# Weighted values of two heads as two 64-column tiles of TensorE, softmax sums from probability tiles that GpSimd adds in pairs

## The reference, cut to what matters

```python
def xattn(q, k, v):                 # q = layernorm(x); k = v = ctx; split in 8 heads of 64
    qn, kn = l2norm(q), l2norm(k)
    sm = softmax(5.0 * einsum('bhdq,bhdk->bhqk', qn, kn), axis=-1)
    return einsum('bhqk,bhdk->bhdq', sm, v)

x = x + xattn(layernorm(x), ctx, ctx)
x = x + experts(layernorm(x))       # top 2 of 4, capacity 512, gelu, two matmuls each
```

## Time and profile before

| | |
|---|---|
| median of 3 runs | 658.95 us (657.25 to 659.49) |
| the profiled execution, its time | 659.4 us |
| its span, first to last instruction | 657.6 us |
| busy: PE, DVE, ACT, POOL | 589.5, 373.2, 300.5, 173.9 us |
| attention | about 6 to 234 us of the span |
| routing, then experts | about 234 to 285 us, then to the end |

### The profile page before, as it was taken

One profiled execution on the slowest core, in us unless ns is written; L12 is line 12 of the kernel. 1 busy time (PEld: TensorE's weight loads), 2 busy tenths in 40 slices (PEclk: granted clock), 3 DMA queues, 4 the chain that ended last, 5 costly groups with the idle time before them and its releaser, 6 DMA issues.

```text
span 657.6 us, 8090 instructions
## 1 busy us (share of the span) xinstructions
PE 589.5 (90%) x2714; PEld 429.0 (65%) x2714; DVE 373.2 (57%) x631; ACT 300.5 (46%) x454; POOL 173.9 (26%) x139
## 2 busy tenths in 40 slices
PE   1999999999999830189999999999999999999994
PEld 1555555565556430168888888888888888888883
DVE  4678888888888798843434443254524344433312
ACT  2687767776777443033434343432424243434310
POOL 4534554355434052261000053000270000320002
PEclk9999999999999965569999999999999999999998
DMA  3512122211210122045131355213272313351001
GB/s 122 175 52 95 64 80 84 92 64 65 91 69 34 64 73 87 17 118 187 64 129 65 115 185 192 84 64 124 99 270 80 128 64 127 130 184 72 1 0 64
DMA packets 39636, 63.62 MB, mean 97 GB/s; under 512 B 3520, under 2 KB 20032, under 8 KB 39616
## 3 DMA queue, kind: packets, MB, share of 16 engines
q1 hardware_dynamic: 35776, 50.78, 22.5%
q0 software_dynamic: 3840, 12.59, 5.5%
HBM read 50.77 MB, written 12.58 MB: 96 GB/s over the span
## 4 chain that ended last, share of the span: by engine, by line
PE 73%; DVE 13%; issue 4%; ACT 2%; POOL 1%; DMA 1%; DVEq 0%; POOLq 0%
PE two L1278 27%; PE two L1144 10%; PE four L1305 9%; PE four L1307 9%; PE four L1308 9%; PE four L1134 4%; DVE p_inv L759 3%; PE bank_t L1161 1%; PE bank_t L1113 1%; DVE junk L923 1%; PE bank_m L1121 1%; DVE o_norm L767 1%; DVE x_all L769 1%; PE bank_t L1153 1%; DVE ss L720 1%
## 5 line engine op out<-in xcount | busy, mean ns | idle before, releaser
L674 ACT ACTIVATE h_f<-two 128x512 f32<-128x512 f32 x64 | 38.3, 599 | 230.1 <-PE two L1278 230.1
L1081 DVE TENSOR_TENSOR h_lo<-h_f,h_hi 128x512 fp32r<-128x512 f32 x64 | 44.1, 690 | 138.7 <-ACT h_hi L675 138.6
L1144 PE MATMUL two<-prob,v_t 128*128 128x512 f32 x256 | 116.7, 598 | 0.0
L1278 PE MATMUL two<-xt_hi,w_hi 128*128 (+1 forms) x256 | 102.7, 401 | 0.3 <-ACT xt_hi L663 0.3
L1278 PE MATMUL two<-xt_hi,w_lo 128*128 (+1 forms) x256 | 101.2, 395 | 0.0
L1278 PE MATMUL two<-xt_lo,w_hi 128*128 (+1 forms) x256 | 100.7, 395 | 0.0
L1305 PE MATMUL four<-w_hi,h_hi 128*128 128x512 f32 x256 | 100.6, 393 | 0.0
L1308 PE MATMUL four<-w_hi,h_lo 128*128 128x512 f32 x256 | 100.5, 393 | 0.0
L1307 PE MATMUL four<-w_lo,h_hi 128*128 128x512 f32 x256 | 100.4, 392 | 0.0
L538 POOL DMA_INDIRECT out<-o_got,idx_all x16 | 19.7, 1232 | 297.6 <-DVE o_got L1095 295.1
L1049 DVE TENSOR_TENSOR w_lo<-raw,w_hi 128x2048 fp32r<-128x2048 f32 x30 | 68.7, 2291 | 22.2 <-ACT w_hi L637 20.0
(11 more groups left out here) (163 smaller groups left out, 727.4 us busy)
## 6 DMA issues: line engine op xcount, KB each, us to landing
raw<-in_L_ffn_W SPq DMA_DIRECT2D x64, 512.0 KB
x_all<-in_x SPq DMA_DIRECT2D x16, 256.0 KB, 2.8
c_sb<-in_ctx SPq DMA_DIRECT2D x16, 256.0 KB, 2.8
out<-x_all SPq DMA_DIRECT2D x16, 256.0 KB, 2.0
x2n_dram<-x2n SPq DMA_DIRECT2D x16, 256.0 KB, 2.1
cst<-in_consts SPq DMA_DIRECT2D x1, 354.5 KB, 4.6
x_got<-x2n_dram,idx_all POOLq DMA_INDIRECT x16
o_got<-out,idx_all POOLq DMA_INDIRECT x16
```

Source lines behind the costliest of these rows:

```text
L674: nc.scalar.activation(h_f[m % 2][:, :], z_ps[m % 2][:, :], ACT.Gelu)
L1081: nc.vector.tensor_tensor(h_lo[m % 2][:, :], h_f[m % 2][:, :], h_hi[m % 2][:, :].bitcast(F32), ALU.subtract).then_inc(h_split, 1)
L1144: last = nc.tensor.matmul(o_ps[h][:, :], v_t[u[1]][:, t, 2 * h:2 * h + 2, :] .rearrange("p a d -> p (a d)"), prob[h][t][:, :], start=(t == ...
L1278: return nc.tensor.matmul(z[:, :], w_part[c][:, w], x_k, start=start, stop=stop)
```

## The change

- The stationary operand of a head is now its 64 columns of values alone. The two heads are two column tiles of TensorE: head 0 writes partitions 0 to 63 and head 1 partitions 64 to 127 of one PSUM bank, `o_ps[0]`. The columns of ones and the memsets that set them are gone.
- GpSimd adds, for each head, probability tiles 0 and 1, then 2 and 3 (`half_sums`, four additions of 128x512 a unit). TensorE multiplies a tile of ones of 64 columns with these (`sums`, four fp32 matmuls a unit) into `o_ps[1]`, at the end of its unit.
- `take_o` is one copy in place of four; `invert_sums` reads PSUM.
- New waits: GpSimd's additions wait for `exp_done` and, into a used buffer, for the last `sums`; `sums` waits for the additions and for the last inversion; ScalarE's exponentials wait for the additions that read the buffer they overwrite. TensorE waits for all constants at its start.
- On GpSimd the additions stand ahead of `key_norms` and behind it, and `query_norms` moves ahead of `key_remainders`.
- Six `tensor_scalar` of VectorE become `scalar_tensor_tensor` with a second tensor operand: both normalisations (a broadcast `rstd`), both `var_e`, both floors.

```diff
+            def half_sums(u, n, reused):
+                pool.wait_ge(exp_done, TT * number(u) + 2 * n + 2)
+                if reused:
+                    pool.wait_ge(sums_ready, number(u))
+                for h in range(2):
+                    last = nc.gpsimd.tensor_tensor(half_sum[h][n][:, :], prob[h][2 * n][:, :],
+                                                   prob[h][2 * n + 1][:, :], ALU.add)
+                last.then_inc(halves_done, 1)
...
             def unit(u, behind, ahead):
+                half_sums(u, 0, behind > 0)
                 if ahead:
...
                     key_norms(after(u))
+                half_sums(u, 1, behind > 0)
                 if ahead > 1:
+                    query_norms(after(after(u)))
                     key_remainders(after(after(u)))
-                    query_norms(after(after(u)))
...
                 if reused:
                     act.wait_ge(pv_done, g - TT + 1)
+                    act.wait_ge(halves_done, 2 * (number(u) - 1) + t // 2 + 1)
...
-                nc.scalar.activation(p_sum[0:DH, :], o_ps[0][DH:P, :], ACT.Copy)
-                nc.scalar.activation(o_sb[0:DH, :], o_ps[0][0:DH, :], ACT.Copy).then_inc(o_taken[0], 1)
-                nc.scalar.activation(p_sum[DH:P, :], o_ps[1][0:DH, :], ACT.Copy).then_inc(sum_taken, 1)
-                nc.scalar.activation(o_sb[DH:P, :], o_ps[1][DH:P, :], ACT.Copy).then_inc(o_taken[1], 1)
+                nc.scalar.activation(o_sb[:, :], o_ps[0][:, :], ACT.Copy).then_inc(o_taken, 1)
...
-                nc.vector.tensor_scalar(var_e[:, :], mv[:, 1:2], LN_EPS, None, ALU.add).then_inc(var_done, 1)
+                nc.vector.scalar_tensor_tensor(var_e[:, :], mv[:, 1:2], LN_EPS, mv[:, 1:2], ALU.add, ALU.max
+                                               ).then_inc(var_done, 1)
...
-                nc.vector.tensor_scalar(x_norm[:, :], x_all[:, bass.ds(n, 1), :].rearrange("p a d -> p (a d)"),
-                                        mv[:, 0:1], rstd[:, 0:1], ALU.subtract, ALU.mult).then_inc(xn_done, 1)
+                nc.vector.scalar_tensor_tensor(x_norm[:, :], x_all[:, bass.ds(n, 1), :].rearrange("p a d -> p (a d)"),
+                                               mv[:, 0:1], rstd[:, 0:1].broadcast_to([P, D]), ALU.subtract, ALU.mult
+                                               ).then_inc(xn_done, 1)
...
-                dve.wait_ge(sum_taken, n + 1)
-                nc.vector.reciprocal(p_inv[:, :], p_sum[:, :]).then_inc(inv_done, 1)
+                dve.wait_ge(sums_ready, n + 1)
+                nc.vector.reciprocal(p_inv[:, :], o_ps[1][:, :]).then_inc(inv_done, 1)
...
                 for h in range(2):
-                    if reused:
-                        pe.wait_ge(o_taken[h], number(u))
-                    last = nc.tensor.matmul(o_ps[h][:, :], v_t[u[1]][:, t, 2 * h:2 * h + 2, :]
-                                            .rearrange("p a d -> p (a d)"), prob[h][t][:, :],
+                    last = nc.tensor.matmul(o_ps[0][DH * h:DH * (h + 1), :], v_t[u[1]][:, t, h, :], prob[h][t][:, :],
                                             start=(t == 0), stop=(t == TT - 1))
                 last.then_inc(pv_done, 1)
+
+            def sums(u, reused):
+                pe.wait_ge(halves_done, 2 * (number(u) + 1))
+                if reused:
+                    pe.wait_ge(inv_done, number(u))
+                for n in range(2):
+                    for h in range(2):
+                        last = nc.tensor.matmul(o_ps[1][DH * h:DH * (h + 1), :], cst[:, C_ONES:C_ONES + DH],
+                                                half_sum[h][n][:, :], start=(n == 0), stop=(n == 1))
+                last.then_inc(sums_ready, 1)
...
             pe.wait_ge(ident_in, 16)
+            pe.wait_ge(cst_in, 16)
...
                 weighted_values(u, 2)
                 weighted_values(u, 3)
+                sums(u, behind > 0)
```

More of the change, by code:

```diff
@@ L178, in xattn_moe_kernel @@
             q_lo = [att(f"q_lo{n}", [P, D], F32R) for n in range(2)]
-            v_t = [att(f"v_t{n}", [P, TT, 4, DH]) for n in range(2)]
+            v_t = [att(f"v_t{n}", [P, TT, 2, DH]) for n in range(2)]
             prob = [[att(f"prob{h}{n}", [P, D]) for n in range(TT)] for h in range(2)]
             o_sb = att("o_sb", [P, D])
-            p_sum = att("p_sum", [P, D])
+            half_sum = [[att(f"half_sum{h}{n}", [P, D]) for n in range(2)] for h in range(2)]
             p_inv = att("p_inv", [P, D])
@@ L262, in xattn_moe_kernel @@
         pv_done = sem("pv_done")
-        sum_taken = sem("sum_taken")
-        o_taken = [sem(f"o_taken{h}") for h in range(2)]
+        halves_done = sem("halves_done")
+        sums_ready = sem("sums_ready")
+        o_taken = sem("o_taken")
         inv_done = sem("inv_done")
@@ L435, in _ @@
             nc.gpsimd.memset(power[:, :], -0.5).then_inc(power_set, 1)
-            for n in range(2):
-                nc.gpsimd.memset(v_t[n][:, :, 1:3, :], 1.0).then_inc(v_ones, 1)
             pool.wait_ge(power_set, 1)
@@ L557, in take_v @@
                     act.wait_ge(pv_done, TT * (n - 1))
-                nc.scalar.activation(v_t[u[1]][:, :, 0:4:3, :],
+                nc.scalar.activation(v_t[u[1]][:, :, :, :],
                                      bank_t[:, :].rearrange("p (t h d) -> p t h d", t=TT, h=2),
@@ L712, in sum_query_squares @@
                 dve.wait_ge(ssq_done, n + 1)
-                nc.vector.tensor_scalar(ss_max[:, 8:16], ss[:, 8:16], NORM_EPS2, None, ALU.max
-                                        ).then_inc(ssq_floor, 1)
+                nc.vector.scalar_tensor_tensor(ss_max[:, 8:16], ss[:, 8:16], NORM_EPS2, ss[:, 8:16], ALU.max, ALU.max
+                                               ).then_inc(ssq_floor, 1)
             def sum_key_squares(u):
@@ L722, in sum_key_squares @@
                 dve.wait_ge(ssk_done, n + 1)
-                nc.vector.tensor_scalar(ss_max[:, 0:8], ss[:, 0:8], NORM_EPS2, None, ALU.max
-                                        ).then_inc(ssk_floor, 1)
+                nc.vector.scalar_tensor_tensor(ss_max[:, 0:8], ss[:, 0:8], NORM_EPS2, ss[:, 0:8], ALU.max, ALU.max
+                                               ).then_inc(ssk_floor, 1)
             def take_logits(u):
@@ L764, in residual @@
                 xu = x_all[:, bass.ds(n, 1), :].rearrange("p a d -> p (a d)")
-                dve.wait_ge(o_taken[1], n + 1)
+                dve.wait_ge(o_taken, n + 1)
                 dve.wait_ge(inv_done, n + 1)
@@ L781, in statistics_x2 @@
                 dve.wait_ge(mv2_done, n + 1)
-                nc.vector.tensor_scalar(var2_e[:, :], mv2[:, 1:2], LN_EPS, None, ALU.add).then_inc(var2_done, 1)
+                nc.vector.scalar_tensor_tensor(var2_e[:, :], mv2[:, 1:2], LN_EPS, mv2[:, 1:2], ALU.add, ALU.max
+                                               ).then_inc(var2_done, 1)
             def normalize_x2(u, reused):
@@ L790, in normalize_x2 @@
                     dve.wait_ge(x2n_stored[u[1]], 16 * u[0])
-                nc.vector.tensor_scalar(x2n[u[1]][:, :], xu, mv2[:, 0:1], rstd2[:, 0:1], ALU.subtract, ALU.mult
-                                        ).then_inc(x2n_done, 1)
+                nc.vector.scalar_tensor_tensor(x2n[u[1]][:, :], xu, mv2[:, 0:1], rstd2[:, 0:1].broadcast_to([P, D]),
+                                               ALU.subtract, ALU.mult).then_inc(x2n_done, 1)
             statistics((0, 0))
@@ L1140, in weighted_values @@
                 pe.wait_ge(exp_done, TT * number(u) + t + 1)
+                if reused:
+                    pe.wait_ge(o_taken, number(u))
                 for h in range(2):
[L1142 to L1145 removed]
+                    last = nc.tensor.matmul(o_ps[0][DH * h:DH * (h + 1), :], v_t[u[1]][:, t, h, :], prob[h][t][:, :],
                                             start=(t == 0), stop=(t == TT - 1))
                 last.then_inc(pv_done, 1)
+            def sums(u, reused):
+                pe.wait_ge(halves_done, 2 * (number(u) + 1))
+                if reused:
+                    pe.wait_ge(inv_done, number(u))
[4 more added lines that the diff above has]
+                last.then_inc(sums_ready, 1)
             def transpose_x2(u):
```

2 lines of the change are left out of this document (removed).

## The result

The changed kernel takes 680.69 us in the median of 4 runs (679.46 to 680.98), the kernel before 658.80 (657.25 to 659.49): a ratio of 1.033, 95% interval 1.031 to 1.035. It is slower by 3.3%; the forecast was 684.4 us, the range 667 to 702. The profiled execution took 679.46 us, with a span of 677.7 (657.6 before).

A forecast was written before the change was run, and what follows sets the result against it. VectorE's loop, with a hand-over through transposes, was taken to bound the kernel, TensorE being nearly full. Terms 19.7 + 4.0 + 0.7 + 0.2 + 0.4 = 25.0 us on the profiled 659.4 gave 684.4 us, range 667 to 702.

The forecast's parts named there:

- start and units to 12: 0.4 us for TensorE's wait for constants, plus 19.7 for twelve units (1 to 12), VectorE's unit growing by 1.64.
- unit 13: End of the attention: x2n and the widening each blocked for 1.2 us by GpSimd's next additions, 1.64 + 2.4 = 4.0.
- unit 14: o_norm blocked 0.97 us, x2n 1.2 + 0.14, against 1.61 of waiting before the inversion that goes: 0.7 together.
- unit 15: Last unit of the attention: 0.2 us; the x2n behind it stays blocked by `w_lo`.
- The loop's three terms: VectorE's unit grows by 0.28 (normalisations) + 0.40 (query floor blocked) + 0.96 (`var_e` blocked) = 1.64 us.
- Part 4: GpSimd's additions block VectorE instructions with two SBUF inputs or old one-tensor form: floor 0.40 us, `var_e` 0.96 by `k_lo`.
- Part 3: Six new VectorE forms: each normalisation from 0.547 to 0.686 us, 0.28 a unit; the small ones no change.
- Part 6: At the start TensorE waits for 354.5 KB of constants: 0.6 to 1.0 us, partly in slack, taken as 0.4.
- A: `var_e` comes ahead of `k_lo`, so the block is lighter: 676.5 us; chance 0.10.
- B: Column tiles don't run side by side, TensorE's unit is 16.5 us: 711, or 690 to 711 if partly overlapped; chance 0.12.
- C: VectorE's q_f and q_hi, one operand in PSUM, are blocked too by the first additions: 700 us; chance 0.08.
- D: New forms pass beside GpSimd's work, x2n behind the last unit under 1 us: 657.2, or 654; chance 0.10.

The follow-up runs named there:

- short additions: Changed kernel with each GpSimd addition covering 64 of 512 columns, the other sums left out: 674.17 us, ratio 1.024.
- old order: Changed kernel with 64-column additions and `key_remainders` back ahead of `query_norms`: 662.33 us, ratio 1.006.
- old forms: Changed kernel with the six `tensor_scalar` back in place of `scalar_tensor_tensor`, additions and order as changed: 678.84 us, ratio 1.031.
- early widening in the kernel before: Kernel before, with query norms widened right behind `statistics_x2` and spread ahead of `values`: 655.14 us, ratio 0.995.
- last experiment: Changed kernel with half the additions, one each side of `key_norms`, query norms widened early, order and forms of before: 646.43 us, ratio 0.982.

## Why the prediction was right

The mechanism held: VectorE's loop set the unit, GpSimd's two-input instructions held it up, and the matmul time saved became waiting. The growth forecast was too large: 25.0 us against 20.1 in the profiled executions and 21.9 in the medians. By parts, in us against before:

| part | forecast | measured, and from what |
|---|---|---|
| start and units to 12 | 0.4 + 19.7 | 17.4: `values` at 210.32 against 192.97 |
| unit 13 | 4.0 | 3.8: 16.4 from logits to logits against 12.6 |
| unit 14 | 0.7 | 1.4: 13.2 against 11.8 |
| unit 15 | 0.2 | -1.5: 7.4 against 8.9 |
| behind the attention | 0 | -0.9: what is left to the span's growth of 20.1 |
| sum | 25.0 | 20.1, of the two profiled executions |

**The loop's three terms.** From start to start, in the mean of the loop's units, `var_e` grew by 0.69 instead of 0.96, the floor by 0.22 instead of 0.40, the two normalisations by 0.21 each instead of 0.14. Together they make 1.33, against 1.64 in the sum; with 0.05 more of waiting for the spread they account for the 1.36 us by which the unit grew. The step that was mis-sized is Part 4's: it counted both blocks whole, from the request to the end of GpSimd's instruction, and didn't take off what the two had needed before (0.15 and 0.17 us in themselves). That put 0.45 too much into the sum, and Part 3 hid 0.14 of it by erring the other way, which is luck. The place, the cause and the margin of `var_e` (0.34 us, 0.31 forecast) were right: the short additions, with the old order and without, show the term by itself. Part 4's rule was too wide at one place: a one-column instruction of the old form isn't blocked (0.15 us with the old forms). So `var_e` is blocked by two parts of the change together, the moved `k_lo` and its own new form. The normalisation took 0.75 us, not the 0.686 of the two-operand row; whether its form or its broadcast operand costs that, no run tells.

**The opening.** Up to `values` at 60.01 and 63.69 the changed kernel lost 3.7 us, as much as Part 6 and two units of 1.64 make. That is luck too: at VectorE's q_f in unit 0 it is 0.36 us ahead (23.71 against 24.07), since a block of x landed earlier (its statistics start at 7.12 against 7.60), and the wait for the constants moves the first transposes only from 6.16 to 6.32. So Part 6's 0.4 isn't there, and unit 0, priced at nothing, costs 0.65 instead. The shortfall is in the loop's ten units, 13.7 instead of 16.4.

**The end.** Unit 13 fell as worked out: x2n lasts 1.20 us longer, the widening 1.06. In unit 14 o_norm and x2n were blocked, but the 1.61 us of waiting that I had set against them came out one unit later, in unit 15: both together -0.1 instead of 0.9. The 0.9 us behind the attention lie between the routing and the first expert: the lag is 21.3 us at VectorE's last count of the routing (263.99 and 285.27) and 20.1 at TensorE's first matmuls on `h_hi` (295.58 and 315.65). Their cause stays open.

**TensorE.** Its pairs of column tiles take the 0.43-us slots, but what a run takes beyond its slots, which I charged with 0.43 for an unpaired one, is about 0.15: 1.87 for four pairs. It changed nothing, since its gain was costed at nothing. Here the reading "VectorE's loop is longer" was thin: by the early widening in the kernel before, the two limits were 0.3 us apart, and a change that freed VectorE would have met TensorE at once.

**The rivals.** A fell: `var_e` came behind the start of `k_lo` and was blocked. B fell: the pairs run side by side. The Trainium skill's rule ("TensorE: Matmul & The Clock Gate", Part 3: Packing small matmuls, The mechanism), that weight loads overlap only in another row group, would by the forecast's working have made rival B's time, an estimate of 711; the eight instructions in 1.87 us show no load in their way, and the measurement decides. C fell: q_f took 0.69 us with additions beside it. The Trainium skill's rule on the port that VectorE and GpSimd share ("SBUF — State Buffer", SBUF: two separate sides) has it so. D fell: the last x2n took 4.97 us in its new form. The granted clock did go down, which the forecast named as a danger, but TensorE had room for it (below).

## What to carry to other kernels

Taking work off the busiest engine gains nothing while a loop through another engine is as long; look for the second limit, and by how little it lies below the first, before you pay for the first. In these runs work given to GpSimd was paid for by VectorE wherever VectorE at the same moment read two SBUF operands, be it one column wide, or ran a copy or a `tensor_scalar` of eight columns or more from SBUF; put such work beside instructions of VectorE that read PSUM, or reductions and inversions, and expect an edit to move the collision rather than to remove it. Here half of the additions, placed so, together with an earlier hand-over gave 1.8%, where the full change cost 3.3%.

## What the runs showed of the hardware

**Column tiles** of 64 columns in the same rows run side by side: 0.43 us for two fp32 instructions of 512 columns, what one takes alone, weight loads included; a run of four such pairs takes 0.15 us more (138.22 to 140.09).

**Who is blocked beside a two-input instruction of GpSimd.** `scalar_tensor_tensor` of one column with two SBUF inputs: 0.96 us, blocked (0.16 elsewhere); `tensor_scalar` of one column: 0.15, not blocked (the old forms, beside `k_lo`); `tensor_scalar` of eight columns: 0.42, blocked (0.17 elsewhere; the last experiment, beside `k_lo`); a copy of 128x512: 1.48, blocked (0.42 elsewhere); two operands with one in PSUM: 0.69, not blocked; the inversion: 3.36 beside the additions, 3.35 with GpSimd idle (at 251.68). So engines don't meet only at semaphores, as is said ahead of the prediction: VectorE and GpSimd also hold each other up with no semaphore between them.

**The clock.** TensorE's granted clock was 1.00 in the loop before, its upper level of 2.4 GHz, and 0.97 after. By windows of 2 us, with the columns of the earlier trace rows:

```profile
164.00:166.00 2.00, 0.42 (x4) 0.00 (x0) 1.92 (x7) 1.18 (x2) 1.43 (x3) 1.00 0.03 11
166.00:168.00 2.00, 1.57 (x10) 1.15 (x12) 0.67 (x3) 0.88 (x2) 2.00 (x3) 0.81 0.34 131
168.00:170.00 2.00, 2.00 (x6) 0.47 (x4) 1.90 (x4) 1.36 (x3) 0.84 (x1) 0.50 0.70 262
```

Behind a wait of some 2 us TensorE ran at 0.50, its lower level of 1.2 GHz, for a few microseconds. It did so behind the waits at 120 and 208 us too, but not behind that at 150 us. It cost the loop nothing that can be seen: the two units with the slow stretches at 123 and 168 us take 14.65 and 14.56 us from q_f to q_f, the loop's mean being 14.66. With the sums issued twice the waits were short, the clock of the window from 60 to 207 us was 1.00 again, and units took 14.60.
